# A routed feed-forward of 56 units that begin at their expert's tokens, each with gathered weights, in place of 64 fixed units

## The reference: a vision block with a top-2 mixture of experts

```python
x = layernorm(h)                                    # 12544 tokens of 192
probs = softmax(x @ Wr); topk_p, topk_i = top_k(probs, 2)
topk_p = topk_p / sum(topk_p)
capacity = ceil(12544 * 2 / 8 * 1.25)               # 3920 slots an expert
order = argsort(-score, axis=1)[:, :capacity]       # an expert keeps its best tokens
dispatch = x[order]                                 # [8, 3920, 192]
out = (silu(dispatch @ w1) * (dispatch @ w3)) @ w2  # inner width 768, per expert
routed[order] += out * weight
shared = (silu(x @ s1) * (x @ s3)) @ s2             # every token
h = h + routed + shared
```

## Time and profile before

| | |
|---|---|
| median of three runs | 3905.7 us |
| profiled execution | 3916.64 us |
| its span, first to last instruction | 3914.8 us |
| attention and routing | to about 2122 us |
| shared units | about 2122 to 2608 us |
| routed units | about 2608 us to the end |
| TensorE busy over the span | 3537.2 us (90%) |
| VectorE, ScalarE, POOL busy | 2483.3, 1703.8, 1427.5 us |
| mean granted TensorE clock | 0.848 |
| DMA | 186.21 MB, 48 GB/s on the mean |

### The profile page before, as it was taken

The page is one execution under the profiler, slowest core; times in us unless marked ns, Lnnn a source line. Parts: engine busy times, 40 slices in busy tenths (PEclk is TensorE's granted clock), DMA queues, the critical chain, the costliest instruction groups (busy, mean ns, idle before and its releaser), DMA issues. The chain is left out here.

```text
span 3914.8 us, 80584 instructions
## 1 busy us (share of the span) xinstructions
PE 3537.2 (90%) x28468; PEld 2523.2 (64%) x28468; DVE 2483.3 (63%) x4827; ACT 1703.8 (44%) x3390; POOL 1427.5 (36%) x1302
## 2 busy tenths in 40 slices
PE   6989889989999998998923999999999999999998
PEld 5766667767677676776712666666666666666665
DVE  5878778777787777877765555554444455345443
ACT  3444444444454444444401444434444444444443
POOL 1222222222222222222221555215555556555555
PEclk7877778777777777787555999999999999999999
DMA  1011111110110101101011222222332323323222
GB/s 67 31 47 39 39 51 34 43 51 26 51 49 28 51 31 46 51 31 47 24 49 48 63 70 71 67 75 35 61 62 39 60 37 62 62 36 61 39 39 32
DMA packets 166708, 186.21 MB, mean 48 GB/s; under 512 B 45263, under 2 KB 145711, under 8 KB 162319
## 3 DMA queue, kind: packets, MB, share of 16 engines
q1 hardware_dynamic: 95696, 123.03, 9.7%
q0 software_dynamic: 57472, 48.46, 8.3%
q10 hardware_dynamic: 13262, 10.65, 0.8%
HBM read 107.75 MB, written 67.85 MB: 45 GB/s over the span
## 5 line engine op out<-in xcount | busy, mean ns | idle before, releaser
L1235 DVE SCALAR_TENSOR_TENSOR ffn_hidden<-ffn_up,ffn_silu 128x490 f32<-128x490 f32 (+2 forms) x534 | 358.2, 672 | 803.9 <-ACT ffn_silu L1218 735.5
L656 POOL TENSOR_TENSOR weights<-weights,x_pair 128x400 f32<-128x400 f32 x384 | 395.6, 1030 | 1243.3 <-DVE weights L521 669.5
L1218 ACT ACTIVATE ffn_silu<-ffn_gate 128x490 f32<-128x490 f32 (+2 forms) x534 | 311.0, 583 | 700.8 <-PE ffn_up L1186 663.6
L570 DVE RECIPROCAL recip<-x_product 128x200 f32<-128x200 f32 x384 | 535.6, 1395 | 0.0
L1203 PE MATMUL ffn_out<-ffn_w_hi,ffn_hidden_hi 128*126 128x192 f16 (+2 forms) x2124 | 522.5, 246 | 0.0
L1205 PE MATMUL ffn_out<-ffn_w_hi,ffn_hidden_lo 128*126 128x192 f16 (+2 forms) x2124 | 522.4, 246 | 0.0
L1204 PE MATMUL ffn_out<-ffn_w_lo,ffn_hidden_hi 128*126 128x192 f16 (+2 forms) x2124 | 522.3, 246 | 0.0
L1391 POOL DMA_INDIRECT out_rows<-done,kept x256 | 426.6, 1666 | 153.7 <-issue 85.3
L1381 POOL DMA_INDIRECT tokens<-dram_x,ids x256 | 279.8, 1093 | 392.8 <-issue 228.5
L1228 DVE TENSOR_TENSOR ffn_hidden_lo<-ffn_hidden,ffn_hidden_hi 128x490 f16<-128x490 f32 (+2 forms) x534 | 355.4, 665 | 8.8
L740 PE MATMUL bank<-w_tok,patches 128*128 128x192 f32 x1536 | 346.1, 386 | 14.1 <-DVE ident L486 14.1
(11 more groups left out here) (185 smaller groups left out, 8074.4 us busy)
## 6 DMA issues: line engine op xcount, KB each, us to landing
patches<-in_patches SPq DMA_DIRECT2D x32, 1176.0 KB, 5.2
ffn_raw<-in_w SPq DMA_DIRECT2D x18, 768.0 KB
dram_x_t<-x_t SPq DMA_DIRECT2D x32, 392.0 KB, 2.5
x_t<-dram_x_t SPq DMA_DIRECT2D x24, 512.0 KB
base<-dram_h SPq DMA_DIRECT2D x24, 384.0 KB
out_rows<-sums ACTq DMA_DIRECT2D x24, 384.0 KB
v_held<-v SPq DMA_DIRECT2D x64, 102.0 KB, 2.3
dram_h<-h SPq DMA_DIRECT2D x32, 192.0 KB
```

Source lines behind the costliest of these rows:

```text
L570: nc.vector.reciprocal(recip[:, n % 2], x_product[:, n % 2]).then_inc(inverted, 1)
L656: nc.gpsimd.tensor_tensor(weights[:, n % 4], weights[:, n % 4], x_pair[:, n % 4, ::-1], ALU.mult)\
L1218: nc.scalar.activation(T.silu[:, m % 2, 0:n], T.gate[m % 2][:, 0:n], ACT.Silu, scale=1.0 / (TOKEN_SCALE * WEIGHT_SCALE)).then_inc(T.silued, 1)
L1235: nc.vector.scalar_tensor_tensor(T.hidden[:, m % 2, 0:n], T.up[m % 2][:, 0:n], HIDDEN_SCALE / (TOKEN_SCALE * WEIGHT_SCALE), T.silu[:, m % ...
```

## The change

The number of routed units falls from 64 to 56. Each has 512 slots, and an expert's first unit begins where its tokens begin: routing rounds each expert's count up to whole units and numbers them one after another, so that which expert a unit belongs to is known only on the chip. `routing` therefore also writes `weights_of`: for each unit the 128 row numbers of its expert's weights.

The weights of all eight experts are split once, during the shared stage: ScalarE's hi parts at the end of unit 2j+1, VectorE's lo parts in the middle of unit 2j+2, for expert j = 0 to 7. SP stores the result to device memory as `front` (hi and lo of w1 and w3, 12288 bytes a row, 1.57 MB an expert) and `back` (hi and lo of w2, 4608 bytes a row, 0.59 MB). Each routed unit then has POOL gather its own front and back by an indirect DMA of 128 rows into one of two buffers. The loop over experts and units becomes one loop over pairs of units. Ids come in one DMA of 4 slots a partition.

```diff
 def expert_units(eng, unit):
-    def expert(e, ws): ...
+    unit(0, 0, 0)
+    unit(1, 0, 1)
+    with eng.Fori(1, XUNITS // 2 - 1) as j:
+        unit(2 * j, j, 0)
+        unit(2 * j + 1, j, 1)
+    unit(XUNITS - 2, XUNITS // 2 - 1, 0)
+    unit(XUNITS - 1, XUNITS // 2 - 1, 1)
...
+XU = 512
+XUNITS = (2 * N + E * (XU - 1)) // XU
...
             # SP, a shared unit
+                if e is not None and slot == 0:
+                    sp.wait_ge(T.weights_lo, 3 * e + 6)
+                    sp.sem_inc(load_spacer, 1)
+                    sp.dma_start(dram["front"][bass.ds(e * 128, 128), :], T.front[1][:]).then_inc(staged, 16)
+                    sp.dma_start(dram["back"][bass.ds(e * 128, 128), :], T.back[1][:]).then_inc(staged, 16)
+                    load_weights(sp, dram, T, e + 1)
...
             # POOL
+            def owned(v, slot):
+                nc.gpsimd.tensor_copy(owner[slot][:], weights_of[:, bass.ds(v, 1)]).then_inc(owner_set, 1)
+                pool.wait_ge(owner_set, v + 1)
+                pool.sem_inc(spacer, 1)
+            def weights(slot, src, dst, landed):
+                nc.gpsimd.indirect_dma_start(
+                    out=dst[:], out_offset=None, in_=dram[src][:, :],
+                    in_offset=bass.IndirectOffsetOnAxis(ap=owner[slot][:], axis=0),
+                    bounds_check=E * 128 - 1, oob_is_err=False).then_inc(landed, 16)
...
+            def routed(v, half, slot):
+                if not among(v, XUNITS - 1):
+                    pool.wait_ge(T.gated, MI * (SHARED + v))
+                    pool.sem_inc(spacer, 1)
+                    if not (isinstance(v, int) and v == 0):
+                        pool.wait_ge(back_in[slot], 16 * (half + slot))
+                        pool.sem_inc(spacer, 1)
+                    owned(v + 1, slot)
+                    weights(slot, "front", T.front[slot], front_in[slot])
...
+                nc.gpsimd.tensor_copy(kept[slot][:], ids[slot][:]).then_inc(ids_kept, 1)
+                if not among(v, XUNITS - 2):
                     pool.wait_ge(turned_full, v + 1)
                     pool.sem_inc(spacer, 1)
                     gather(v + 2, half + 1, slot)
+                if not among(v, XUNITS - 1):
+                    pool.wait_ge(T.out_full, 2 * (SHARED + v))
+                    pool.sem_inc(spacer, 1)
+                    weights(slot, "back", T.back[slot], back_in[slot])
...
             # TensorE
+            def back_of(v, half, slot):
+                pe.wait_ge(back_in[1 - slot], 16 * half + 16)
+                tensor_out(nc, pe, T, SHARED + v, 1 - slot, 1 - slot, WHOLE)
+            def routed(v, half, slot):
                 g = SHARED + v
+                pe.wait_ge(front_in[1 - slot], 16 * half + 16)
+                tensor_unit(nc, pe, T, g, 1 - slot, XU)
...
             # ScalarE, at the end of a shared unit
+                if e is not None and slot == 1:
+                    act.wait_ge(staged, 32 * e + 32)
+                    act.wait_ge(T.raw_in, 48 * e + 96)
                     weights_hi(nc, T, 1)
...
             # VectorE, after the third step of a shared unit
+                def remainders():
+                    dve.wait_ge(T.weights_hi, 3 * e + 6)
+                    weights_lo(nc, T, 1)
```

More of the change, by code:

```diff
@@ L860, in routing @@
         rank = sb("rank", [128, E])
-        base = sb("base", [128, E])
+        ones = sb("ones", [128, 128])
+        row = sb("row", [128, 1])
+        numbers = sb("numbers", [128, XUNITS])
+        ended = sb("ended", [128, XUNITS, E])
+        owner = sb("owner", [128, XUNITS])
+        rounded = sb("rounded", [128, E], I32)
+        units = sb("units", [128, E])
+        ends = sb("ends", [128, E])
         place = sb("place", [128, E])
@@ L878, in routing @@
         block = ctx.enter_context(nc.Block())
-        constants = ((rank, "rank"), (same, "same"), (before, "before"), (base, "base"))
+        constants = ((rank, "rank"), (same, "same"), (before, "before"), (row, "row"), (numbers, "numbers"))
         @block.sync
@@ L1068, in _ @@
                 ts(slots[:, :, c], best[:], float(SLOTS), None, ALU.add)
+            tt(ended[:], numbers[:].unsqueeze(2).to_broadcast([128, XUNITS, E]),
+               ends[:].unsqueeze(1).to_broadcast([128, XUNITS, E]), ALU.is_ge)
+            step(nc.vector.tensor_reduce(owner[:], ended[:], AX.X, ALU.add))
+            ts(owner[:], owner[:], float(E - 1), None, ALU.min)
+            ts(weights_of[:], owner[:], 128.0, row[:, 0:1], ALU.mult, ALU.add)
 TOKEN_SCALE, WEIGHT_SCALE, HIDDEN_SCALE = 2.0 ** 6, 2.0 ** 6, 2.0 ** 4
@@ L1239, in vector_unit @@
             lo(m - 1)
+        if m == 2 and between:
+            between()
     lo(MI - 1)
@@ L1254, in expert_units, with among, ffn @@
 def expert_units(eng, unit):
[L1257 to L1284, removed]
+    unit(0, 0, 0)
[5 more added lines that the diff above has]
+    unit(XUNITS - 1, XUNITS // 2 - 1, 1)
+def among(v, first):
+    return isinstance(v, int) and v >= first
+def ffn(nc, dram, T, slot_of, entry, weights_of):
     with ExitStack() as ctx:
@@ L1481, in split, with put @@
                 tokens_hi(nc, T, turned[0][:, 0:XU], turned[1][:, 0:XU], XU)
-            def put(v, half, slot, first):
-                if not first:
+            def put(v, half, slot):
+                if not (isinstance(v, int) and v < 2):
                     act.wait_ge(scattered[slot], 64 * half)
@@ L1491, in put, with unit @@
                     act.wait_ge(T.out_full, 2 * g + n + 1)
[L1492 removed]
+                    for c in range(2):
                         t = 2 * n + c
[L1494 to L1495 removed]
+                        last = nc.scalar.activation(done[slot][:, t, :], T.out[n][:, c * D:(c + 1) * D],
+                                                    ACT.Copy, scale=kept[slot][:, t, 1:2].bitcast(F32))
                     last.then_inc(T.out_used, 1)
             split_shared(0, 0, ST)
[L1500 removed]
+            def unit(g, half, slot, tiles, e=None):
                 scalar_unit(nc, act, T, g, slot, columns_of(tiles))
```

187 lines of the change are left out of this document (87 added, 100 removed).

## The result

The changed kernel takes 4095.9 us (median of 4 runs, 4088.6 to 4122.8), the kernel before 3901.3 us on the same chip (3883.0 to 3907.6): 1.0519 times, 95% interval 1.0457 to 1.0582.

A forecast was written before the change was run, and what follows sets the result against it. TensorE bounds the old routed stage; POOL, at 23.1 us a unit, the new one. 3914.8 + 12 (routed) + 130 (shared) - 5 + 3 + 1 = 4055.8 us span, brought to the runs' median: 4045 us, range 3880 to 4170.

The forecast's parts named there:

- POOL, not TensorE, paces the routed units: Routed stage: POOL's cycle 23.1 us a unit against TensorE's 20.2, so +12 us in place of -147.
- rival D: Routed stage: POOL pays by the byte to issue long-row gathers; 25.3 us a unit, 4168 us; chance 0.09.
- The quiet cycle: Routed stage: POOL's time per unit with no delay of the id load, 19.9 us.
- The id load's delay: Routed stage: next ids, loaded right behind the front gather on the same DMA engines, come 3.2 us late (0 to 3.95).
- Rival A: Routed stage: the id load slips in beside the front gather, TensorE paces at 20.2 us; 3888 us; chance 0.16.
- x_t stands behind 4.3 MB in SP's queue: Shared stage: x_t waits behind store and raw loads, idling TensorE 7.7 us a pair (0 to 10).
- Rival B: Shared stage: x_t isn't held up by store and raw loads; 3963 us, slower by 1.5%; chance 0.11.
- Two short stalls a pair: Shared stage: ScalarE's and VectorE's weight splits, apart, stall TensorE 2.4 and 3.4 us, 5.8 a pair (0 to 8.11).
- The clock: Shared stage: half clock for 5.4 us after each idle for x_t loses 2.7 us a pair (0 to 8.1).
- Routing: Before the shared stage: routing gains ten small VectorE steps, +3 us.
- unit 24: First routed unit's start: its 8.11 us idle goes, its own gather is next late; -5 us (0 to -9).
- rival C: Both stages: neither the ids nor x_t are held up; 3804 us, faster by 2.6%; chance 0.14.

The follow-up runs named there:

- e1: Changed kernel with POOL copying the ids before it issues the gather of front, instead of after; 3943.7 us, 1.0091 times before.
- e2: Changed kernel with front gathers of units 2 to 53 cut to 256-byte rows, order and instruction count unchanged (wrong weights); 3896.8 us, one run.
- e4: Changed kernel with raw loads behind the store cut to 64 columns, 0.1 MB for 2.16 MB (wrong weights); 4041.3 us, one run.
- e3: Changed kernel with SP loading x_t of unit 2j+3 before waiting for the lo parts, ahead of store and raw loads; 4004.1 us, 1.0256 times before.
- e7: Changed kernel with the edits of e3, e5 and e6 together; 3806.7 us, 0.9734 times before.
- e9: Changed kernel with the edits of e3, e5 and e8 together; 3780.1 us, 0.9682 times before.
- e6: On top of e1, POOL copies the weights' row numbers before waiting for the scatter, so front goes out earlier; 3936.6 us, 1.0093 times before.
- e5: On top of e3, ScalarE's and VectorE's weight splits are spread in pieces between steps instead of one block each; 3952.5 us, 1.0130 times before.
- e8: On top of e6, POOL gathers front two units ahead, once the current unit's gates are through; 3912.8 us, one run.

## Why the prediction was right, and where it was off

**POOL, not TensorE, paces the routed units: right.** The forecast was 23.1 us a unit; it is 23.54. POOL in one unit of after, which answers to the earlier trace rows, then the page's front gathers and id loads with the median us from the start of the issue to the landing, in after and (last) the id loads in e1, and what ran in the DMA engines of after from 3044.3 to 3048.1:

```profile
3040.97 0.80 POOL L1407 COPY owner<-weights_of 128x1 uint32 x1
3042.71 1.09 POOL L1413 DMA_INDIRECT ffn_front<-dram_front,owner  x1 [0.94 <-POOL owner L1407]
3043.81 0.20 POOL L1451 COPY kept<-ids 128x8 uint32<-128x8 uint32 x1
3050.99 1.07 POOL L1400 DMA_INDIRECT tokens<-dram_x,ids  x1 [6.98 <-DMA ids<-dram_table]
...
3056.27 1.00 POOL L1413 DMA_INDIRECT ffn_back<-dram_back,owner  x1 [0.30 <-issue]
3057.57 1.61 POOL L1423 DMA_INDIRECT out_rows<-done,kept  x1 [0.30 <-issue]
...
ffn_front<-dram_front,owner POOLq DMA_INDIRECT x56, 7.2
ids<-dram_table SPq DMA_DIRECT2D x56, 4.0 KB, 5.8
...
ids<-dram_table SPq DMA_DIRECT2D x56, 4.0 KB, 1.6
...
q0 software_dynamic: 104, 1.28, 96.3%
```

POOL waits 6.98 us for the next ids. Front and back take it 1.09 and 1.00 us to issue, so rival D (it pays by the byte) is refuted, which e2 repeats. The quiet cycle is slightly better than said: e2's 20.2 less 0.7 of waiting for ScalarE (37.6 / 52) is 19.5, not 19.9. The id load's delay is larger: 7.0 - 2.8 = 4.2 us, and by the landings 5.8 - 1.6 = 4.2 as well, not 3.2 and just over the bound of 3.95. 19.5 + 4.2 = 23.7. 55 times 0.44 make the 24 us between +36 and +12. I had taken off a part of front's 3.8 us; in truth front moved at 313 GB/s (1.56 MB between 3044 and 3049), slower than the 411 I took, and the id load came behind all of it. It was issued at 3044.26, yet no packet of its queue starts before 3048.19 (in the last row front's queue has the engines alone), and in 54 of the units it lands 0.17 to 0.18 us after front. Rival A (it slips in) is refuted by that and by e1 and e2.

TensorE's idle before a unit is 2.4 us on the mean and not the 2.9 forecast, though the pitch is longer: of the 185 us by which the stage is longer than e2's, 126 are idle and 59 the lower clock, which fills time that TensorE would otherwise have spent waiting.

**x_t stands behind 4.3 MB in SP's queue: right, and the agreement to the tenth is luck.** 7.7 us of idle were forecast; over the eight pairs it is 5.6 to 9.2 us, 7.6 on the mean. The nine waits above hold the kernel's first two for x_t and seven of these; the tenth follows, 83.5 us in all. Both moments whose difference the idle is came later than forecast: counted from the unit's first matmul, TensorE was through at 27.3 us on the mean (forecast 24.7) and had the next tokens at 34.9 (32.4). SP's queue, which answers to the earlier trace rows:

```profile
2491.79 0.37 SPq L1354 DMA_DIRECT2D dram_front<-ffn_front  x1
2492.34 0.37 SPq L1355 DMA_DIRECT2D dram_back<-ffn_back  x1
2492.92 3.55 SPq L1151 DMA_DIRECT2D ffn_raw<-in_w  x3
2497.07 0.60 SPq L1341 DMA_DIRECT2D x_t<-dram_x_t  x1
```

VectorE was through at 2491.5 and x_t went out at 2497.07, behind the five other DMAs. e4 takes 5.1 us off by bytes alone and e3 takes the wait away. Rival B is refuted by both.

**Two short stalls a pair: right.** 5.8 forecast, 5.5 measured in after and 5.3 in e3 on the mean, single ones 2.3 to 3.3 us (2.3 and 2.4 in the pair below), where the forecast had 2.4 and 3.4.

**The clock: this term was mis-sized.** Forecast 2.7 us a pair, with 8.1 as the upper end "if the two shorter stalls do it as well". They often do. TensorE's first matmul behind each of the three idles of one pair, and the windows that follow or begin in the idle (clock: third number from the end), which answer to the earlier trace rows:

```profile
2481.49 0.39 PE L1205 MATMUL ffn_gate<-ffn_tokens_near_hi,ffn_front 128*128 128x512 f16 x1 [2.26 <-DVE ffn_hidden L1258]
...
2492.21 0.39 PE L1205 MATMUL ffn_gate<-ffn_tokens_near_hi,ffn_front 128*128 128x512 f16 x1 [2.38 <-DVE ffn_hidden L1258]
...
2508.99 0.60 PE L1205 MATMUL ffn_gate<-ffn_tokens_near_hi,ffn_front 128*128 128x512 f16 x1 [6.83 <-DVE ffn_tokens_far L1189]
```

```profile
2482.64:2486.05 3.41, 3.41 (x10) 1.22 (x9) 0.70 (x2) 1.10 (x2) 2.35 (x3) 0.50 0.02 1
2492.89:2496.30 3.41, 3.41 (x11) 1.47 (x10) 1.25 (x2) 0.23 (x1) 0.97 (x1) 0.50 1.00 404
2506.54:2513.36 6.82, 4.37 (x11) 1.62 (x12) 2.41 (x4) 0.87 (x2) 4.03 (x4) 0.50 0.29 72
```

The granted clock is 0.50, 1.2 of 2.4 GHz, over all three, 13.65 us in this pair. Not every short idle does this: over the eight pairs the clock fell at all eight long idles (61.4 us at 0.50) and at 11 of the 16 short ones (41.0 us); the idle of 3.03 us that ends at 2323.35 was not among them. Of the 102.4 us TensorE was busy in 73.6, and the rest lay in idles (in the third window above it is busy 4.37 of 6.82 us). Half of 73.6 is 36.8, or 4.6 us a pair. The pair costs (599.5 - 456.8) / 8 = 17.8, and less 5.5 and 7.6 that leaves 4.8, which agrees. Of the 4.6 about 2.1 follow the long idles, where 2.7 were forecast, and 2.5 the short ones, where nothing was. 8 x (17.8 - 16.2) = 13 us are the difference of +143 and +130. The choice that failed was to let only the long idle count.

**The rest.** Routing +3.6 (+3) and unit 24 -4.2 (-5) are within a microsecond. The tail is +6.4, not +1: behind the last split unit 55 still waits 2.9 us for its front, and 20.2 us of the tail are at half clock, against 15.8 in e2 (2.2 us). In e1 and e2 unit 55 has no such wait, and they take 50.7 and 50.8 us from the last split to the end, where after takes 55.2.

**The sum.** The forecast lay 51 us under the median. By stages it is 24 for the id load, 13 for the clock, 5 for the tail and 1 elsewhere: 43.5, the difference of +184.5 and +141. Of the other 7 the rounding of 4047 to 4045 is 2, and 5 lie between the profiled execution and the median (26.9 less the 21.5 of attention).

Had the change been judged by its columns alone, it should have won 2.6% (rival C). It had such a gain in it (2.7% in e7, 3.2% in e9): it was hidden by where four things stood in the instruction streams, the ids, x_t, the splits and front, and not by the arithmetic.

## What to carry to other kernels

A small load on which an engine waits must be issued ahead of the large transfer, not behind it: here four kilobytes behind 1.57 MB cost 148 us, by the order of two steps. When a move is off the critical path, follow the queue that it enters and ask what is issued next on it, and also whether the engine that issues it closes a chain with the bounding engine's own work: the chain of e6 runs over two units and no single wait shows its length. Several microseconds of block work on a side engine can be free in pieces where each piece is about as long as the gap of a step (here 0.94 to 1.35 us against 0.87) and the bounding engine has a lead (e5). A low clock on an engine that does not set the pace costs nothing there (59 us in the routed stage of after), while the stalls of an engine that does set it cost twice, in idle and in clock.

## What the runs showed of the hardware that was not expected

- Idles of TensorE of 2.3 to 3.3 us went along with 3.41 us or more at a granted clock of 0.50 in 11 of 16 cases in after and in 8 of 16 in e3; behind the others of the same length the clock stayed at full speed.
- A 4 KB load issued on SP's queue 1.5 us behind the gather of 1.57 MB on POOL's landed 0.17 to 0.18 us after that gather in 54 units of after; issued ahead of it in e1, it landed after 1.6 us.
- POOL's issue of an indirect DMA of 128 rows took 1.09 us for 12288-byte rows and 1.10 for 256-byte rows.
- Between a copy by POOL and the indirect DMA behind it stand 0.94 to 0.96 us of idle in the rows of after, e1, e2 and e6 (1.01 in e8's), though in e6 and e8 the copy's result was not what the DMA used.
- Behind the store of 2.16 MB, three raw loads held SP 3.55 us, with 2.16 MB and with 0.1 MB alike; with no store ahead it was 1.73 us.
